# Score products of two heads against zero-padded low keys, and one buffer for the turned attention output

## The chip, the cores and the metric

One core of one Trainium2 chip. The metric is the device time of one execution of the kernel in microseconds (us). In the profile, PE is TensorE (PEld its weight loads), DVE is VectorE, ACT is ScalarE, POOL is GpSimd and SP (SPq its queue of DMA issues) is SyncE.

## What is computed

Two transformer layers over x of 4 sequences, 256 tokens, 256 channels, in fp32. Each layer adds an attention and an FFN, both of the layer norm of the same x:

```python
x = L0_attn_seq
xn = _layernorm(x, axis=-1)
x = x + _L0_attn_ref(xn, ...) + _L0_ffn_ref(xn, ...)
xn = _layernorm(x, axis=-1)
x = x + _L1_attn_ref(xn, L1_attn_w_qkv, L1_attn_w_o) + _L1_ffn_ref(xn, L1_ffn_w_fc, L1_ffn_w_proj)
```

The layer-1 attention is where the change is. It has 32 query heads and 4 key heads of 64 channels:

```python
qkv = jnp.einsum('bsh,oh->bso', hidden_states, w_qkv).reshape(b, s, HQ + 2 * HKV, D)
q, k = _rope(q, pos), _rope(k, pos)                 # x1*cos - x2*sin, x2*cos + x1*sin
k, v = jnp.repeat(k, rep, axis=2), jnp.repeat(v, rep, axis=2)
scores = jnp.einsum('bqhd,bkhd->bhqk', q, k) * D ** (-0.5)
scores = jnp.where(causal[None, None], scores, jnp.finfo(scores.dtype).min)
attn = jax.nn.softmax(scores, axis=-1)
out = jnp.einsum('bhqk,bkhd->bqhd', attn, v).reshape(b, s, HQ * D)
return jnp.einsum('bso,ho->bsh', out, w_o)
```

## The kernel before, in words

**Split numbers.** TensorE multiplies in fp32r, which keeps fewer bits than fp32. So each operand is held as a high part (rounded to fp32r) and a low part (the rest), and products are made of hi·hi, lo·hi and hi·lo. For the scores the two parts of a query lie above each other in 128 partitions: `qT[i]` holds, for each of the 8 heads of a key group, 64 rows of high and 64 rows of low queries. `kT[b % 2]` holds each key head twice above each other, once as high (s = 0) and once as low keys (s = 1). One product with s = 0 gives (q_hi + q_lo)·k_hi, one with s = 1 gives (q_hi + q_lo)·k_lo.

**Units.** The layer-1 attention runs over 16 iterations (batch i // 4, key group i % 4), each with 8 heads and two halves of 128 query tokens. An iteration has 6 units of one score bank (512 columns): u = 0, 1, 4, 5 have two heads of the second half of the queries and 256 keys; u = 2, 3 have four heads of the first half, which by causality need only the first 128 keys. `scores(n)` (line 1232) makes 4 products of 256 columns for a second-half unit and 8 products of 128 columns for a first-half unit (line 1250), and then one mask product (line 1253). The mask is added by a bf16 product with the identity.

**What follows a unit.** DVE takes the negated maxima (line 911), ACT the exponentials in place with their sums (line 515), DVE divides (lines 921 and 927), PE turns the probabilities (line 1004), ACT and DVE split them (lines 524 and 933), PE multiplies them with the values (line 1287) into one bank, ACT and DVE split that (lines 529 and 939) into `oT`, and `project_out` (line 1291) multiplies it with the output weights (line 1307). Every engine has its order written out by `slot(n)`: PE's slot has the scores of unit n, the turning of unit n-2, a group of value products, at u = 0, 3 (and 4 for keys and values) the projection of a coming block ("fill"), and at u = 1 and 5 the output projection of the iteration before. The two halves of `oT` are written from group products in slots u = 4, 5 of the same iteration and u = 0, 2 of the next. Before the change `oT` has a buffer for even and one for odd iterations.

**How queries and keys get ready.** A block is half an iteration's queries (4 heads, two heads above each other in 128 partitions, 2 x 256 columns) or a batch's keys. PE projects it (line 1200), ACT copies it to `raw` (line 490), SP turns the halves of each head with 4 transfers into `turned` (lines 357 and 358), POOL multiplies with cos and sin (`rope_products`, lines 658 and 660) and makes high sum, full sum and low part (`rope_sums`, lines 668 to 670), SP places them by transfers: 4 for a query block (line 378), 8 for a key block (line 381, since keys stand twice). SP's loop is: turn block n+1, then place block n. POOL's list (lines 676 to 702) has between the blocks the low parts of the layer-1 weights (line 606), two a block until block 7, and in the FFN the inverse roots (line 592). The blocks in order are k(0), q(0,0), q(0,1), q(1,0), q(1,1), q(2,0), q(2,1), q(3,0), k(1), q(3,1), q(4,0) and so on; q(i,0) is needed by unit (i,0), q(i,1) by unit (i,3), k(b) by the first unit of batch b. k(b+1) is filled in unit 4 of a batch's second iteration, the values in unit 4 of its third.

**Memory.** Buffers are placed by hand in SBUF; many share their place with others that are dead by then. `probT_hi` lies at 104K, `rope_a` and `rope_b` have two halves of 2 KB each, `split_hi` and `split_lo` too.

**The stages in time.** Layer 0 and the layer-1 norms to about 40 us, the layer-1 FFN to about 90 us (ten steps; blocks are filled in steps 0, 1, 3, 4, 6), attention from there, with units (0,0) and (0,1) inside the FFN's last steps.

Of the kernel before, what the change touches and what calls it, by code (L numbers as in the profile page):

```python
# [7 lines left out]
F32 = mybir.dt.float32  # L8
F32R = mybir.dt.float32r
# [5 lines left out]
P = 128  # L15
# [50 lines left out]
def build(nc, seq, w_qkv0, w_out0, pm, w_ffn0, bias0, w_qkv1, w_o1, w_fc, w_proj, vec, const, out):  # L66
    with ExitStack() as ctx:
# [36 lines left out]
        def at(name, offset, shape, dt=F32):  # L104
# [23 lines left out]
        oT = [[at(f"oT{i}_{w}", k * K + 4 * K * j, [P, 4, SEQ], F32R) for j, w in enumerate(("hi", "lo"))]  # L128
              for i, k in enumerate((148, 64))]
# [7 lines left out]
        probT = [at(f"probT_{w}", k * K, [P, 4, 512], F32R) for w, k in (("hi", 104), ("lo", 112))]  # L137

        yT_full = at("yT_full", 156 * K, [P, B, 512])
        split = [at(f"split_{w}", 156 * K + 4 * K * i, [P, 2, 2, SEQ], F32R) for i, w in enumerate(("hi", "lo"))]  # L140

        rope_a = at("rope_a", 164 * K, [P, 2, 512])
        rope_b = at("rope_b", 168 * K, [P, 2, 512])
# [17 lines left out]
        ones_r = at("ones_r", 185 * K, [P, P], F32R)  # L161
        wcol = at("wcol", 186 * K, [P, DIM])
        idle_in = at("idle_in", 187 * K, [P, 512], BF16)
# [30 lines left out]
        v_zero = sem("v_zero")  # L194
# [48 lines left out]
        def moves(n):  # L243
            return 8 if BLOCKS[n][0] == "k" else 4
# [49 lines left out]
        def group_place(it, i):  # L294

            c, j = unit_heads(GROUPS[i][0])[0], 2 * (i // 2)
            return [w[:, j:j + 2, P * c:P * c + P] for w in oT[it % 2]]
# [29 lines left out]
        def _(sp):  # L327
# [32 lines left out]
            def place_heads(n):  # L360
# [37 lines left out]
        def _(act):  # L398
# [45 lines left out]
            act.wait_ge(ld["cst"], 16)  # L444
            nc.scalar.activation(ones_r[:, :], cst[:, C_ONE:C_ONE + P], ACT.Copy).then_inc(ones_done, 1)
# [106 lines left out]
            for step in range(STEPS):  # L552
# [25 lines left out]
        def _(pool):  # L578
# [8 lines left out]
            pool.wait_ge(zeroed, 3)  # L587

# [62 lines left out]
            def rope_products(n):  # L651
# [4 lines left out]
                whole, half, a, z = (t[:, n % 2, :].rearrange("p (j t) -> p j t", j=2) for t in (raw, turned, rope_a, rope_b))  # L656
                pool.wait_ge(raw_done, n + 1)
                pool.tensor_tensor(a, whole, cos, ALU.mult)  # L658
# [727 lines left out]
```

## Time and profile before

| | us |
|---|---|
| three timed runs: median, lowest, highest | 386.6, 385.39, 388.68 |
| the profiled execution itself | 387.23 |
| its span, first to last instruction | 385.4 |
| PE, DVE, POOL, ACT busy | 369.0, 307.1, 279.4, 250.0 |
| mean granted clock of TensorE | 0.996 |

Durations below are of the profiled execution. Matmuls overlap in the records, so the mean duration of one (some 280 ns) is not its pace; the pace is read from the start of one group to the start of the next. An "idle before" names what ended the wait. SPq rows are DMA issues, not the transfers.

### The profile page before, as it was taken

How to read it: one execution, taken by the hardware profiler on the slowest of the kernel's cores; microseconds unless marked ns; L12 is line 12 of the kernel's file. 1: busy time of each engine (PE TensorE's matmuls, PEld its weight loads, DVE VectorE, ACT ScalarE, POOL GpSimd, SP SyncE). 2: the span in 40 equal slices, each digit the busy share in tenths (PEclk: the TensorE clock that was granted, in tenths of full speed). 3: DMA queues.
4: the chain of work that ended last, by engine and by line, in shares of the span. 5: the costliest groups of instructions: out<-in, count | busy, mean ns of one | idle time of the engine just before them, and what ended most of it. 6: DMA issues, size and time to landing. Idle time of an engine off the chain costs nothing.

```text
span 385.4 us, 8456 instructions
## 1 busy us (share of the span) xinstructions
PE 369.0 (96%) x2888; PEld 343.6 (89%) x2888; DVE 307.1 (80%) x684; ACT 250.0 (65%) x804; POOL 279.4 (72%) x238
## 2 busy tenths in 40 slices
PE   8998889989999998999999999999999999999995
PEld 3667779979899997999999999999999999998985
DVE  6878999876999885779777888787788879788882
ACT  1368855573987764667667676757666667767671
POOL 3437759789999996977779897667997777776000
PEclk9999999999999999899999999999999999999999
DMA  7996112513444345443345643334565343333300
GB/s 261 414 408 284 27 30 55 138 43 81 110 99 96 79 108 130 112 109 80 87 110 120 157 110 92 93 92 98 131 149 142 93 104 83 84 83 86 79 2 27
DMA packets 34219, 45.15 MB, mean 117 GB/s; under 512 B 5505, under 2 KB 25986, under 8 KB 33794
## 3 DMA queue, kind: packets, MB, share of 16 engines
q1 hardware_dynamic: 34032, 44.62, 43.1%
q8 instruction: 23, 0.38, 0.4%
q14 instruction: 18, 0.15, 0.1%
q10 hardware_dynamic: 146, 0.00, 0.0%
HBM read 13.14 MB, written 1.05 MB: 37 GB/s over the span
## 4 chain that ended last, share of the span: by engine, by line
PE 67%; POOL 15%; DVE 9%; SPq 3%; DMA 2%; ACT 2%; issue 2%; POOLq 0%
PE bank L1287 14%; PE bank L1250 11%; PE bank L1307 10%; PE bank L1004 10%; PE bank L1200 10%; PE bank L1253 3%; POOL woT_lo L606 3%; POOL rope_a L669 2%; POOL split_lo L670 2%; POOL split_hi L668 2%; POOL rope_b L660 2%; PE bank L1013 2%; DMA wq0T<-in_L_attn_w_qkv_dram 2%; PE bank L1159 2%; POOL rope_a L658 2%
## 5 line engine op out<-in xcount | busy, mean ns | idle before, releaser
L515 ACT ACTIVATE bank<-bank,neg_max 128x256 f32<-128x256 f32 (+1 forms) x256 | 101.3, 397 | 10.0 <-DVE neg_max L911 9.9
L524 ACT ACTIVATE probT_hi<-bank 128x512 fp32r<-128x512 f32 x96 | 57.6, 600 | 73.6 <-PE bank L1004 73.4
L911 DVE TENSOR_REDUCE neg_max<-bank 128x2 f32<-128x512 f32 (+1 forms) x96 | 65.9, 687 | 31.2 <-PE bank L1253 30.9
L1287 PE MATMUL bank<-probT_hi,v 128*128 128x256 f32 x384 | 76.4, 295 | 0.6 <-DVE oT_lo L939 0.6
L660 POOL TENSOR_TENSOR rope_b<-turned,cst 128x512 f32<-128x512 f32 x36 | 47.1, 1308 | 40.6 <-DMA turned<-raw 40.6
L1250 PE MATMUL bank<-kT,qT 128*128 128x256 f32 (+1 forms) x512 | 73.4, 276 | 1.7 <-DMA qT<-split_lo 1.7
L927 DVE TENSOR_TENSOR prob<-bank,rsum 128x512 f32<-128x512 f32 x96 | 66.4, 691 | 3.3
L1250 PEld LDWEIGHTS bank<-kT,qT 128*128 128x128 f32 x512 | 66.5, 191 | 1.9 <-DMA qT<-split_lo 1.9
L933 DVE TENSOR_TENSOR probT_lo<-bank,probT_hi 128x512 fp32r<-128x512 f32 x96 | 65.4, 681 | 0.5 <-ACT probT_hi L524 0.4
L1287 PEld LDWEIGHTS bank<-probT_hi,v 128*128 128x128 f32 x384 | 58.6, 189 | 3.5 <-issue 2.2
L1004 PE MATMUL bank<-cst,prob 128*128 128x128 f32 x384 | 58.4, 275 | 2.2 <-DVE prob L927 2.2
L1287 PE MATMUL bank<-probT_lo,v 128*128 128x256 f32 x192 | 54.1, 282 | 0.0
L515 ACT ACTIVATION_READ_ACCUMULATOR bank<-bank,neg_max 128x1 f32 x256 | 53.6, 210 | 0.0
L1004 PEld LDWEIGHTS bank<-cst,prob 128*128 128x128 f32 x384 | 46.1, 142 | 5.5 <-DVE prob L927 3.1
L670 POOL TENSOR_TENSOR split_lo<-rope_a,split_hi 128x512 fp32r<-128x512 f32 x36 | 46.3, 1286 | 2.8
L668 POOL TENSOR_TENSOR split_hi<-rope_a,rope_b 128x512 fp32r<-128x512 f32 x36 | 46.2, 1284 | 2.6
L669 POOL TENSOR_TENSOR rope_a<-rope_a,rope_b 128x512 f32<-128x512 f32 x36 | 47.0, 1306 | 0.0
L658 POOL TENSOR_TENSOR rope_a<-raw,cst 128x512 f32<-128x512 f32 x36 | 46.4, 1290 | 0.0
L939 DVE TENSOR_TENSOR oT_lo<-bank,oT_hi 128x256 fp32r<-128x256 f32 x64 | 27.2, 425 | 17.6 <-ACT oT_hi L529 17.3
L1287 PEld LDWEIGHTS bank<-probT_lo,v 128*128 128x128 f32 x192 | 36.3, 189 | 0.0
L1253 PE MATMUL bank<-mask_b,ident_b 128*128 128x256 bf16 (+1 forms) x96 | 30.8, 321 | 0.0
L1200 PE MATMUL bank<-xT_hi,qkvT_hi 128*128 128x256 f32 x144 | 30.7, 295 | 0.0
(158 smaller groups left out, 735.2 us busy)
## 6 DMA issues: line engine op xcount, KB each, us to landing
turned<-raw SPq DMA_DIRECT2D x144, 64.0 KB, 2.0
qT<-split_hi SPq DMA_DIRECT2D x64, 128.0 KB, 2.4
qT<-split_lo SPq DMA_DIRECT2D x64, 128.0 KB, 2.4
wq0T<-in_L_attn_w_qkv_dram SPq DMA_DIRECT2D x4, 512.0 KB, 7.9
wout<-in_L_attn_w_out_dram SPq DMA_DIRECT2D x4, 512.0 KB, 12.4
nat_qkv<-in_L_attn_w_qkv_dram SPq DMA_DIRECT2D x2, 1024.0 KB, 20.5
nat_o<-in_L_attn_w_o_dram SPq DMA_DIRECT2D x1, 2048.0 KB, 21.4
kT<-split_hi SPq DMA_DIRECT2D x16, 128.0 KB, 2.4
```

Of the source, the lines that this page charges most:

```text
L515: ins = nc.scalar.activation(own, own, ACT.Exp, bias=neg_max[it % 2][:, first + j:first + j + 1], accum_out=sums[it % 2][:, first + j:firs ...
L524: nc.scalar.activation(probT[0][:, n % 4, :], bank[2 + n % 2][:, :], ACT.Copy).then_inc(t_hi, 1)
L658: pool.tensor_tensor(a, whole, cos, ALU.mult)
L660: own_done(pool.tensor_tensor(z, half, sin, ALU.mult))
L669: own_done(pool.tensor_tensor(a, a, z, ALU.add))
L911: dve.tensor_reduce(neg_max[n // UNITS % 2][:, unit_columns(n % UNITS)], score_bank(n)[:, :].rearrange("p (h k) -> p h k", h=heads), AX.X, ...
L927: dve.tensor_tensor(a, e, share, ALU.mult).then_inc(s_norm, 1)
L933: dve.tensor_tensor(lo, bank[2 + n % 2][:, :], hi.bitcast(F32), ALU.subtract).then_inc(t_lo, 1)
L1004: ins = pe.transpose(ps[:, P * j:P * j + P], a, ident)
L1200: ins = pe.matmul(bank[place][:, SEQ * j:SEQ * j + SEQ], qkvT[w][:, k, at:at + P], xT[s][:, k, SEQ * b:SEQ * b + SEQ], start=i == 0, stop= ...
L1250: pe.matmul(ps[:, keys * j:keys * j + keys], qT[it % 2][:, h + j, P * c:P * c + P], kT[b % 2][:, g, s, 0:keys], start=j == 0 and s == 0, s ...
L1287: ins = pe.matmul(group_bank(), v[b % 2][:, DH * z:DH * z + P], p, start=m == 0, stop=m == last)
```

## The change

Four of the eight products of a first-half unit (those with the low keys, s = 1) go. In their place stand two products of 256 columns: the stationary operand is `q_hi`, the high queries of two heads above each other as the rope leaves them, the moving one `k_pad`, which for z = 0 has the low keys in rows 0 to 63 and zeros below, and for z = 1 zeros above and the low keys in rows 64 to 127. So 128 columns come out for each of the two heads. The product of low queries with low keys is left out in first-half units.

For that `rope_sums` writes the high queries into `q_hi[it % 2]` instead of `split_hi`; POOL waits before it until the scores that read the old ones are done. The key blocks get 4 more transfers (12 in all), which place the low keys of the first 128 tokens in `k_pad`. POOL zeroes each `k_pad` once with two fills (`pad(0)` at the start, `pad(1)` behind the FFN's last root). PE waits for the zeroing in first-half units of the first two batches. `rope_a`, `rope_b` and `split_hi` have one buffer, and `rope_products` waits for the low part of the block before. `oT` has one buffer, `probT_hi` moves to 64K, and `ones_r` (moved from ScalarE's early work to FFN step 3), `wcol` and `idle_in` get other places.

```diff
-        oT = [[at(f"oT{i}_{w}", k * K + 4 * K * j, [P, 4, SEQ], F32R) for j, w in enumerate(("hi", "lo"))]
-              for i, k in enumerate((148, 64))]
+        oT = [at(f"oT_{w}", (148 + 4 * j) * K, [P, 4, SEQ], F32R) for j, w in enumerate(("hi", "lo"))]
+        q_hi = [at(f"q_hi{i}", k * K, [P, HG // 2, SEQ], F32R) for i, k in enumerate((168, 104))]
+        k_pad = [at(f"k_pad{i}", k * K, [P, HKV, 2, P], F32R) for i, k in enumerate((184, 108))]
...
-        probT = [at(f"probT_{w}", k * K, [P, 4, 512], F32R) for w, k in (("hi", 104), ("lo", 112))]
+        probT = [at(f"probT_{w}", k * K, [P, 4, 512], F32R) for w, k in (("hi", 64), ("lo", 112))]
...
-        split = [at(f"split_{w}", 156 * K + 4 * K * i, [P, 2, 2, SEQ], F32R) for i, w in enumerate(("hi", "lo"))]
-
-        rope_a = at("rope_a", 164 * K, [P, 2, 512])
-        rope_b = at("rope_b", 168 * K, [P, 2, 512])
+        split_hi = at("split_hi", 156 * K, [P, 2, SEQ], F32R)
+        split_lo = at("split_lo", 158 * K, [P, 2, 2, SEQ], F32R)
+        rope_a = at("rope_a", 164 * K, [P, 2, SEQ])
+        rope_b = at("rope_b", 166 * K, [P, 2, SEQ])
...
         def moves(n):
-            return 8 if BLOCKS[n][0] == "k" else 4
+            return 12 if BLOCKS[n][0] == "k" else 4
...
                 for w in range(2):
-                    for s in range(2):
-                        src = split[s][DH * w:DH * w + DH, n % 2, :, :].bitcast(F32)
+                    own = slice(DH * w, DH * w + DH)
+                    low = split_lo[own, n % 2, :, :].bitcast(F32)
+                    if what == "q":
+                        high = q_hi[it % 2][own, 2 * half:2 * half + 2, :].bitcast(F32)
+                    else:
+                        high = split_hi[own, :, :].bitcast(F32)
+                    for s, src in enumerate((high, low)):
                         if what == "q":
                             sp.dma_start(qT[it % 2][DH * s:DH * s + DH, 4 * half + w:4 * half + 4:2, :].bitcast(F32), src).then_inc(placed[n % 2], 16)
                         else:
                             for z in range(2):
                                 sp.dma_start(kT[b % 2][DH * z:DH * z + DH, w:HKV:2, s, :].bitcast(F32), src).then_inc(placed[n % 2], 16)
+                    if what == "k":
+                        for z in range(2):
+                            sp.dma_start(k_pad[b % 2][DH * z:DH * z + DH, w:HKV:2, z, :].bitcast(F32), low[:, :, 0:P]).then_inc(placed[n % 2], 16)
...
-            act.wait_ge(ld["cst"], 16)
-            nc.scalar.activation(ones_r[:, :], cst[:, C_ONE:C_ONE + P], ACT.Copy).then_inc(ones_done, 1)
...
+                if step == WCOL_STEP - 2:
+                    act.wait_ge(ld["cst"], 16)
+                    act.wait_ge(lo0_done, B)
+                    nc.scalar.activation(ones_r[:, :], cst[:, C_ONE:C_ONE + P], ACT.Copy).then_inc(ones_done, 1)
...
+            def pad(i):
+
+                for z in range(2):
+                    own = k_pad[i][DH * (1 - z):DH * (1 - z) + DH, :, z, :]
+                    pool.memset(own.bitcast(F32), 0.0).then_inc(pad_zero, 1)
+                    pool.wait_ge(pad_zero, 2 * i + z + 1)
+
+            pool.wait_ge(v_zero, 2)
+            pool.wait_ge(blk_done, 1)
+            pad(0)
...
                 pool.wait_ge(raw_done, n + 1)
-                pool.tensor_tensor(a, whole, cos, ALU.mult)
+                if n:
+                    pool.wait_ge(split_done, n)
+                pool.tensor_tensor(rope_a[:, :, :], whole, cos, ALU.mult)
...
-                hi, lo = (t[:, n % 2, :, :] for t in split)
+                a, z, lo = rope_a[:, :, :], rope_b[:, :, :], split_lo[:, n % 2, :, :]
+                if BLOCKS[n][0] == "k":
+                    hi = split_hi[:, :, :]
+                else:
+                    _, it, part = BLOCKS[n]
+                    hi = q_hi[it % 2][:, 2 * part:2 * part + 2, :]
+                    if it >= 2:
+                        pool.wait_ge(s_full, (it - 2) * UNITS + 3 + part)
...
             tile_root(7)
+            pool.wait_ge(root_out, TILES + B + 2)
+            pad(1)
             rope_products(3)
...
                 c, heads, h, keys = unit_heads(u)
+                if c == 0 and n < HKV * UNITS * 2:
+                    pe.wait_ge(pad_zero, 2 * (b + 1))
                 for j in range(heads):
-                    for s in range(2):
+                    for s in range(c + 1):
                         pe.matmul(ps[:, keys * j:keys * j + keys], qT[it % 2][:, h + j, P * c:P * c + P], kT[b % 2][:, g, s, 0:keys],
                                   start=j == 0 and s == 0, stop=False, skip_group_check=True)
+                    if c == 0 and j % 2:
+                        pe.matmul(ps[:, keys * (j - 1):keys * (j + 1)], q_hi[it % 2][:, (h + j) // 2, 0:P], k_pad[b % 2][:, g, :, :],
+                                  start=False, stop=False, skip_group_check=True)
```

## Rows read from the trace of the kernel before

**Rows 1.** The page: busy shares, and two of its costliest groups.

```profile
PE 369.0 (96%) x2888; PEld 343.6 (89%) x2888; DVE 307.1 (80%) x684; ACT 250.0 (65%) x804; POOL 279.4 (72%) x238
...
L1250 PE MATMUL bank<-kT,qT 128*128 128x256 f32 (+1 forms) x512 | 73.4, 276 | 1.7 <-DMA qT<-split_lo 1.7
...
L670 POOL TENSOR_TENSOR split_lo<-rope_a,split_hi 128x512 fp32r<-128x512 f32 x36 | 46.3, 1286 | 2.8
```

**Rows 2.** Busy time of each engine in two stretches.

```profile
134.00:144.00 10.00, 10.00 (x86) 9.83 (x86) 8.74 (x18) 6.62 (x25) 9.76 (x8) 1.00 0.46 107
...
200.00:220.00 20.00, 20.00 (x172) 19.68 (x171) 16.51 (x34) 13.49 (x48) 17.61 (x15) 1.00 0.57 133
```

**Rows 3.** Chain of waits in order of time: start, duration, what.

```profile
137.61 1.31 POOL split_lo L670
...
138.94 0.65 SPq L381
...
144.29 0.57 SPq L357
...
145.54 1.72 SPq L357
...
150.02 2.36 DMA qT<-split_lo
...
152.42 1.14 PE bank L1250 x8
...
168.74 0.84 PE bank L1250 x8
...
186.16 0.84 PE bank L1250 x8
```

**Rows 4.** Timeline of TensorE around the gap.

```profile
150.44 0.28 PE L1287 MATMUL bank<-probT_lo,v 128*128 128x256 f32 x1
152.42 1.14 PE L1250 MATMUL bank<-kT,qT 128*128 128x128 f32 x8 [1.71 <-DMA qT<-split_lo]
...
157.03 0.64 PE L1250 MATMUL bank<-kT,qT 128*128 128x256 f32 x4
```

**Rows 5.** Stretch behind the gap; granted clock behind POOL's busy time.

```profile
153.30:156.80 3.50, 3.50 (x19) 3.30 (x18) 2.14 (x4) 1.89 (x9) 3.49 (x3) 0.51 0.35 82
```

**Rows 6.** Timeline of all engines, iteration 7.

```profile
217.59 0.64 PE L1250 MATMUL bank<-kT,qT 128*128 128x256 f32 x4
...
218.07 0.28 PE L1253 MATMUL bank<-mask_b,ident_b 128*128 128x256 bf16 x1
...
223.26 1.01 PE L1250 MATMUL bank<-kT,qT 128*128 128x128 f32 x8
...
224.10 0.39 PE L1253 MATMUL bank<-mask_b,ident_b 128*128 128x512 bf16 x1
...
227.61 0.68 DVE L911 TENSOR_REDUCE neg_max<-bank 128x4 f32<-128x512 f32 x1
```

**Rows 7.** Timeline of TensorE, iteration 14, behind its first-half units.

```profile
353.50 0.66 PE L1004 MATMUL bank<-cst,prob 128*128 128x128 f32 x4 [0.69 <-DVE prob L927]
```

**Rows 8.** Timeline of GpSimd, start and end of the FFN.

```profile
1.78 0.52 POOL L581 MEMSET probT<- 1x512 f32 x1
...
10.86 3.45 POOL L592 TENSOR_TENSOR tok<-tok,neg_half 128x8 f32<-128x8 f32 x2 [6.48 <-DVE tok L750]
...
79.84 0.54 POOL L592 TENSOR_TENSOR ffac<-ffac,neg_half 128x1 f32<-128x1 f32 x1 [1.70 <-DVE ffac L717]
```

**Rows 9.** Timeline of SyncE's queue: last issues of q(4,0) and q(7,1).

```profile
156.63 0.62 SPq L378 DMA_DIRECT2D qT<-split_lo  x1
...
219.17 0.61 SPq L378 DMA_DIRECT2D qT<-split_lo  x1
```

**Rows 10.** Timeline of TensorE: scores of units (4,0) and (7,3).

```profile
162.91 0.64 PE L1250 MATMUL bank<-kT,qT 128*128 128x256 f32 x4
...
226.20 1.01 PE L1250 MATMUL bank<-kT,qT 128*128 128x128 f32 x8
```

More of the change, by code:

```diff
@@ L160, in build @@
         pmT = at("pmT", 184 * K, [P, 2, 2, HC])
-        ones_r = at("ones_r", 185 * K, [P, P], F32R)
-        wcol = at("wcol", 186 * K, [P, DIM])
-        idle_in = at("idle_in", 187 * K, [P, 512], BF16)
+        ones_r = at("ones_r", 162 * K, [P, P], F32R)
+        wcol = at("wcol", 163 * K, [P, DIM])
+        idle_in = at("idle_in", 136 * K, [P, 512], BF16)
         abs_out = at("abs_out", 164 * K, [P, FF // P * DIM])
@@ L193, in build @@
         out_full, out_added = sem("out_full"), sem("out_added")
-        v_zero = sem("v_zero")
+        v_zero, pad_zero = sem("v_zero"), sem("pad_zero")
         raw_done, rope_done, split_done = sem("raw_done"), sem("rope_done"), sem("split_done")
@@ L296, in group_place @@
             c, j = unit_heads(GROUPS[i][0])[0], 2 * (i // 2)
-            return [w[:, j:j + 2, P * c:P * c + P] for w in oT[it % 2]]
+            return [w[:, j:j + 2, P * c:P * c + P] for w in oT]
         def group_bank():
@@ L655, in rope_products @@
                 cos, sin = (cst[:, a:a + SEQ].rearrange("p (j t) -> p j t", j=1).to_broadcast([P, 2, SEQ]) for a in (at, at + SEQ))
-                whole, half, a, z = (t[:, n % 2, :].rearrange("p (j t) -> p j t", j=2) for t in (raw, turned, rope_a, rope_b))
+                whole, half = (t[:, n % 2, :].rearrange("p (j t) -> p j t", j=2) for t in (raw, turned))
                 pool.wait_ge(raw_done, n + 1)
-                pool.tensor_tensor(a, whole, cos, ALU.mult)
+                if n:
+                    pool.wait_ge(split_done, n)
+                pool.tensor_tensor(rope_a[:, :, :], whole, cos, ALU.mult)
                 pool.wait_ge(turn_landed[n % 2], 64 * (n // 2 + 1))
-                own_done(pool.tensor_tensor(z, half, sin, ALU.mult))
+                own_done(pool.tensor_tensor(rope_b[:, :, :], half, sin, ALU.mult))
             def rope_sums(n):
@@ L665, in rope_sums @@
                     has_landed(pool, n - 2)
-                a, z = (t[:, n % 2, :].rearrange("p (j t) -> p j t", j=2) for t in (rope_a, rope_b))
-                hi, lo = (t[:, n % 2, :, :] for t in split)
+                a, z, lo = rope_a[:, :, :], rope_b[:, :, :], split_lo[:, n % 2, :, :]
[6 more added lines that the diff above has]
+                        pool.wait_ge(s_full, (it - 2) * UNITS + 3 + part)
                 pool.tensor_tensor(hi, a, z, ALU.add)
@@ L1306, in project_out @@
                             final = g == HKV - 1 and half == 1 and e == 1 and (s, w) == (0, 1) and j == 3
-                            ins = pe.matmul(bank[BANK_OUT][:, DIM * e:DIM * e + DIM], oT[it % 2][s][:, j, e:e + 2 * P - 1:2],
+                            ins = pe.matmul(bank[BANK_OUT][:, DIM * e:DIM * e + DIM], oT[s][:, j, e:e + 2 * P - 1:2],
                                             woT[w][:, 4 * g + j, :], start=first, stop=final, skip_group_check=True)
```

## The prediction

> **What bounds the kernel now.** I read the page's busy shares first, then the chain that ended last, then the stretches, then the timelines of the one place where the chain changes engine. A unit is written (i,u): iteration i of 16 (batch i//4, key group i%4), u from 0 to 5; k(b) and q(i,half) are the blocks that the rope prepares.
>
> TensorE (PE) is busy 96% of the span [rows 1], and in the steady stretch all of it: 20.00 of 20 us from 200 to 220 [rows 2]. But the chain has three parts. Up to 80 us it is the FFN. From 80 us to 139 us it is GpSimd (POOL): 9.76 of 10 us busy in 134 to 144 [rows 2], no pause longer than the 0.07 us between a result and its reader, because the rope of each block (five operations of 1.29 us [rows 1]) and two weight splits of the same size take some 9.2 us, while PE makes a block each 8.7 us (half of 186.16 - 168.74, one iteration [rows 3]). Its last link is k(1)'s split, which ends at 138.92. Then the SyncE queue (SP) issues eight transfers of k(1), four turns, and the four of q(3,1), and only when the last of these lands does PE go on: 150.02 + 2.36 = 152.4 [rows 3]. PE's preceding product started at 150.44 and the scores of (3,3) at 152.42, after 1.71 us of idling [rows 4]; that is the only time in 512 score products that PE waited for queries [rows 1]. From 152.4 on the chain is PE itself.
>
> Behind that gap the granted clock was 0.51 from 153.3 to 156.8, about the lower level of 1.2 GHz [rows 5], and PE's pace is the full one again from 157.03 [rows 4]: 3.4 us at half speed, which lost about 1.7 us. So a microsecond saved on PE ahead of 150 is eaten by the gap, one saved behind it counts, and one added to POOL from 86 us on or to SP in 139 to 150 is paid in full.
>
> **The change, part by part.**
>
> *Products.* A first-half unit (u = 2, 3; two per iteration, 32 in all) has eight score products of 128 columns. They run from 223.26 to 224.10, when the mask product starts: 0.84 us, 105 ns each [rows 6]. A product of 256 columns takes 120 ns: four from 217.59 to 218.07 [rows 6]. After the change a unit has four of 128 and two of 256: 4 x 105 + 2 x 120 = 660 ns, 0.18 us less. Bounds: if all six run at 120 ns it is 0.12, if all at 105 it is 0.21. No row shows 128- and 256-column products mixed; I take 0.18, since the weight load of the next product can lie beside a longer stream.
> The Trainium skill, TensorE: Matmul & The Clock Gate, section LDWEIGHTS, gives a weight load as columns/1.2 ns, an estimate of 107 ns for 128 columns, and under Back-to-back issue gap 109 ns for a warm 256-column product alone. By that the unit would save 0.21 us, the upper bound; the 120 ns of the row speak for less.
>
> Of the 32 units, 7 stand ahead of the gap: (0,2) to (3,2). They save 1.3 us, and PE then waits that much longer. 25 stand behind it: 25 x 0.18 = 4.5 us. Two of these, (14,3) and (15,3), have no projection beside them, and PE waits there for VectorE's normalising anyway (0.69 us at 353.50 [rows 7]); I drop them: -0.4. VectorE is close in first-half slots too: its maxima at 227.61 start without a pause behind the oT work [rows 6]. I give 0.3 us of the gain back for that. Left: 3.8 us (bounds 2.3 and 5.2).
>
> *k_pad zeroing.* Two fills of 64 partitions x 512 numbers per buffer. A fill of 512 numbers per partition took 0.52 us [rows 8]; with 0.07 behind each and 0.07 for the wait on the root: 1.2 us per pad (bounds 0.7, if a fill takes half of that row, and 2.2, if it takes double; spans on POOL are rough). pad(0) lies in POOL's idle 6.48 us before 10.86 [rows 8]: nothing. pad(1) stands behind the last root, at 86 us, in the stretch where POOL is the chain: +1.2 in full. Behind it on POOL are all ropes and weight splits to k(1), and for these SP and PE wait.
>
> *Four more transfers per k block.* Eight issues take SP from 138.94 to 144.29, 0.67 us each [rows 3]: +2.7 us per k block. For k(0) this shifts the turn of q(0,1), before a stretch where POOL idles 1.70 us until 79.84 [rows 8]: nothing. For k(1) the four stand ahead of the turn of q(4,0) and of q(3,1)'s placing, on the chain: +2.7 in full (bounds 2.5 and 3.8, the latter with a further slow issue). One of the four turn issues took 1.72 us [rows 3], 1.1 more than the others, a hitch that few issues have; it has even odds to fall elsewhere: -0.5.
>
> *Clock.* PE's idle time before (3,3) grows from 1.7 to 1.7 + 1.2 + 2.7 + 1.3 - 0.5 = 6.4 us. A half-clock stretch behind it is there already; how it falls can change its price from 1.7 to between 0.8 and 3.4. I take no change, and keep -0.9 and +1.7.
> The same page of the skill, section Terms, prices it as throttled time x (1 - K/N): 3.4 x 0.5 = 1.7 us, as the row shows; its rule that idle PE loses the clock speaks against this change, since by it a longer gap never costs less than a gap too short to lose it.
>
> *Without a price.* One oT buffer: the heads of iteration i are written behind PE's own products of its slot, and the reader of the old ones (the output projection of i-1) is issued on PE before them in (i,1) and (i,5); no wait is new. rope_a and rope_b single: POOL runs in order, the added wait is for its own last operation, 0.07 us, and between 86 and 139 us a weight split lies between. q_hi as the source and its wait on scores: those units were issued before the fill whose block is roped. ones_r on ScalarE moves from beside PE's work to step 3 of the FFN, behind a wait of ScalarE's for PE. probT_hi over the spent projT: its first write follows the last projection on PE. Waits on pad_zero: set long before.
>
> *Later blocks.* q(4,0)'s last issue is at 156.63, its landing some 2.4 later at 159.0, its scores at 162.91 [rows 9, 10]: 3.9 us to spare, and SP and PE shift together. q(7,1), behind k(2), is issued last at 219.17, lands at 221.6, and is needed at 226.20 [rows 9, 10]: 4.6 us to spare, of which the four issues take 2.7 and PE's three faster units on the way 0.5. 1.4 us stay; the like holds behind k(3).
>
> **Sum** against the profiled execution's own 387.23 us (span 385.4, 1.8 around it): + 1.2 + 2.7 - 0.5 - 3.8 = -0.4, so 386.8. That execution is 0.6 above the median of the three timed runs (386.6), so 386.2.
>
> **Rivals.**
> 1. *The preparation hides* (the gap does not grow): 25 units of 0.18 count and neither fills nor issues do: 386.6 - 4.5 = 382.1. For it: q blocks other than q(3,1) landed in time. Against: POOL has no pause from 86 to 139, and SP issues back to back from there to 150.
> 2. *The queue starves PE at each new batch* (the other side): behind k(2) and k(3) the spare 1.4 us are used up as well. It decides from 1.4 us on, for instance by one slow issue and a later k split. Each gap then costs some 1 us and up to 1.7 of clock: 386.2 + 2 x 2.7 = 391.6. For it: the slack of 4.6 is measured and 3.2 of it go. Against: 1.4 us is more than one hitch of 1.1.
> 3. *The products don't pay*: a 256-column product among 128s costs as much as two of them, and the unit saves nothing. Then 386.6 + 1.2 + 2.7 - 0.5 = 390.0. Against: 120 against 2 x 105 ns in the rows.
>
> **How the numbers follow.** Forecast 0.65, its own range 383.0 to 388.8 (gain 2.3 to 5.2, pad 0.7 to 2.2, clock -0.9 to +1.7, not all at once). Rival 1: 0.18; rival 2: 0.08; rival 3: 0.09. 1% is 3.9 us, about what a measurement of this kernel tells from no change: faster is below 382.7, slower above 390.5. Rival 1 gives nearly all of faster, with a little of the forecast: 0.18. Rival 2 and nearly half of rival 3 give slower: 0.12. Same: 0.70. The range reaches down to rival 1 and up towards rival 3: 382.0 to 390.0.
>
> **What would show it.** Right: eight-product score groups of first-half units become six in 0.66 us; twelve kT and k_pad issues behind k(1)'s split, which ends near 140.1; (3,3) starting at 155 to 156.5 behind 5 to 7 us of idle PE, then half clock; a period of 17.0 instead of 17.4 us afterwards; no gap at (7,3) and (11,3). Wrong: (3,3) near 152, or a PE gap in front of another unit, or no shorter period.

## The result: 0.9% slower, and where the time went

The changed kernel takes 390.17 us (median of 20 runs, 387.27 to 393.82); the kernel before took 386.56 us beside it (20 runs, 385.05 to 388.68). The ratio is 1.0092, with a 95% interval of 1.0073 to 1.0111; one execution of the changed kernel, more than 1.5% above its fastest (393.82), is left out of the ratio. The forecast was 386.2 us with a range from 382.0 to 390.0. The profiled execution took 391.75 us, its span is 389.9 us, 4.5 more than before; it is 1.6 us above the median of the twenty, so what is read from it below explains the longer ones among them.

The page of the changed kernel: busy time of the engines, the granted clock over the span, the chain by engine, and the group of the score products.

```profile
span 389.9 us, 8377 instructions
...
PE 365.6 (94%) x2808; PEld 339.6 (87%) x2824; DVE 307.5 (79%) x684; ACT 250.6 (64%) x804; POOL 282.1 (72%) x242
...
PEclk9999999999999998799999999999999899999999
...
POOL 40%; PE 32%; issue 12%; DVE 8%; SPq 3%; ACT 2%; DMA 1%; POOLq 0%
...
L1284 PE MATMUL bank<-kT,qT 128*128 128x256 f32 (+1 forms) x384 | 63.7, 275 | 7.4 <-DMA qT<-split_lo 7.4
```

PE is busy 3.4 us less than before [rows 1] and the span is longer. The last line says why: PE idled 7.4 us for placed queries where it idled 1.7 before [rows 1]. The clock row has two dents. PE's waits for queries in the changed kernel, from the view of waits (us in total, times, longest):

```profile
PE bank L1284 <- DMA qT<-split_lo: 7.4, 3, 5.1
```

Three waits instead of one, and the timeline of PE in the changed kernel shows them at (3,3), (7,3) and (11,3), each the first unit that reads the query block placed behind a k block:

```profile
149.84 0.28 PE L1324 MATMUL bank<-probT_lo,v 128*128 128x256 f32 x1
155.25 0.69 PE L1284 MATMUL bank<-kT,qT 128*128 128x128 f32 x2 [5.13 <-DMA qT<-split_lo]
...
228.82 0.44 PE L1284 MATMUL bank<-kT,qT 128*128 128x128 f32 x2 [0.20 <-DMA qT<-split_lo]
...
301.96 0.44 PE L1284 MATMUL bank<-kT,qT 128*128 128x128 f32 x2 [2.04 <-DMA qT<-split_lo]
```

Setting each unit's first score product against the same unit of the kernel before gives a ledger (both from the timeline of PE; shift = after - before, us):

```
unit          before   after    shift   what happened since the row above
(3,2)         147.62   147.18   -0.44   cheaper products ahead of the gap
(3,3)         152.42   155.25   +2.83   idle 5.13 instead of 1.71
(3,4)         157.03   160.41   +3.38   more of it at half clock
(7,2)         223.26   225.69   +2.43   six first-half units cheaper
(7,3)         226.20   228.82   +2.62   idle 0.20, (7,2) cheaper
(11,2)        295.36   296.98   +1.62   cheaper products
(11,3)        298.30   301.96   +3.66   idle 2.04
(12,0)        307.11   312.24   +5.13   half clock behind (11,3)
(15,5)        371.36   375.52   +4.16   cheaper products
```

So up to (11,2) the change goes nearly as forecast: each first-half unit earns 0.16 us behind the gap, and (7,3) loses 0.35. A gap costs 0.15 us more than the idle time says (at (3,3) before, (7,3) and (11,3)), since the records of products overlap. At (11,3) all that was earned behind (3,4) is lost again and more. The clock behind the first gap, in windows of the changed kernel (length, then busy time and count of PE, PEld, DVE, ACT and POOL, the granted clock, DMA share and GB/s):

```profile
153.00:155.20 2.20, 0.00 (x0) 0.00 (x0) 0.00 (x0) 0.00 (x0) 2.12 (x3) 0.59 0.84 194
155.20:160.00 4.80, 4.75 (x21) 4.46 (x22) 2.14 (x4) 1.76 (x8) 4.58 (x4) 0.50 0.40 93
```

The clock fell while PE was still idle, and stayed at its lower level (1.2 GHz) for about 6.8 us in all, until 160.0. From (3,3) to (3,4) the kernel before took 4.61 us and this one 5.16. Behind (11,3) it is about 3.4 us of half clock, and the shift grows by 1.5 from there to (12,0).

How often the clock falls differs between executions. A stretch of 3.4 us at half clock takes 0.004 off the mean granted clock of a span of 385 us. Of 75 executions of the kernel before that ran beside the experiments, 41 have 0.998 or more, so no such stretch, and a median of 385.3 us; 22 have 0.995 or 0.996 like the profiled one (387.1), and 12 have 0.991 (388.4). Of the changed kernel's twenty none is above 0.991: ten lie at 0.989 to 0.991 (mean 388.6 us), which leaves room for little more than the 6.8 us at (3,3), and ten at 0.983 to 0.987 (391.5 us, the profiled one among them), which have a further stretch.

**The chain at (3,3).** POOL first, in the changed kernel: the two fills, then the first rope behind them, and k(1)'s last split.

```profile
86.05 1.09 POOL L604 MEMSET k_pad<- 64x512 f32 x2
87.22 1.30 POOL L682 TENSOR_TENSOR rope_a<-raw,cst 128x512 f32<-128x512 f32 x1
...
138.51 1.29 POOL L700 TENSOR_TENSOR split_lo<-rope_a,split_hi 128x512 fp32r<-128x512 f32 x1
```

The rope starts 1.19 later than before (86.03); the split ends at 139.80 instead of 138.91, +0.89. Then the queue of SP:

```profile
139.83 1.33 SPq L387 DMA_DIRECT2D kT<-split_hi  x2
...
145.13 1.73 SPq L387 DMA_DIRECT2D kT<-split_lo  x2
146.90 1.27 SPq L390 DMA_DIRECT2D k_pad<-split_lo  x2
148.27 0.57 SPq L358 DMA_DIRECT2D turned<-raw  x1
...
152.87 0.62 SPq L384 DMA_DIRECT2D qT<-split_lo  x1
```

Twelve issues take 8.44 us where eight took 5.35 [rows 3]: four more at 0.65, and one slow one (the pair at 145.13 takes 1.73). The slow turn of [rows 3] is gone (-1.1). The last issue is 2.85 later than the 150.02 of [rows 3], and the scores follow it.

**The chain at (7,3).** The last placing of q(7,1) is issued at 225.09, 5.92 us later than before [rows 9], while PE stands 2.43 later. Its time from issue to landing, in the changed kernel and in the one before:

```profile
DMA to landing us min/median/max: 3.7/3.7/3.7
```

```profile
DMA to landing us min/median/max: 3.4/3.4/3.4
```

Before the change it landed at 222.6 and was needed at 226.20: 3.6 us to spare. The queue takes 5.92 - 2.43 = 3.5 of that and the landing 0.3 more, so PE waits 0.2.

**The chain at (11,3).** The same queue, first in the changed kernel:

```profile
284.76 2.11 SPq L387 DMA_DIRECT2D kT<-split_hi  x2
...
298.11 0.61 SPq L384 DMA_DIRECT2D qT<-split_lo  x1
298.77 1.90 SPq L400 DMA_DIRECT2D out_dram<-x  x1
```

and in the kernel before:

```profile
290.96 0.61 SPq L378 DMA_DIRECT2D qT<-split_lo  x1
291.62 0.60 SPq L391 DMA_DIRECT2D out_dram<-x  x1
```

The last placing is issued 7.15 us later while PE stands only 1.62 later. Three parts can be read: the four issues (2.6), a slow issue in the first pair (2.11 against 1.33, 0.8), and k(3)'s split, whose end moved from 280.96 to 284.73. The split is late because the turned half of q(11,0) landed late. The timeline of POOL in the changed kernel:

```profile
272.81 1.28 POOL L684 TENSOR_TENSOR rope_b<-turned,cst 128x512 f32<-128x512 f32 x1 [3.44 <-DMA turned<-raw]
```

In the kernel before it started at 269.22, behind 2.30 us of idling. The last turn of q(11,0) was issued at 267.13 before and at 269.25 after; those 2.1 us are nearly PE's own shift there (1.9), and the other 1.5 passed between this issue and its landing. From there the lateness runs on through two blocks: the split +3.77, the four issues and the slow one +3.4, together the 7.15.

And the placed queries land later: the times from issue to landing of q(11,1)'s last placings, in the changed kernel and in the one before, are

```profile
DMA to landing us min/median/max: 2.7/3.3/3.8
```

```profile
DMA to landing us min/median/max: 2.3/2.5/2.6
```

The store of batch 1's output (line 400) is issued 0.66 us behind the last placing in both kernels; the last placing issued at 298.11 lands at 301.9, 3.8 later. Before, it was issued at 290.96, landed 2.6 later at 293.6 and was needed at 298.30: 4.7 us to spare. The queue takes 7.15 - 1.62 = 5.5 of that and the landing 1.2, in all 6.7: 2.0 us short, which is the gap.

### The profile page after: what moved, and what is told of

Same layout as the page of the kernel before. It is cut to its first block, busy times and chain, and to the rows that moved or that the text cites. A ratio compares the mean times of both kernels' runs of the same rounds, so it can differ in the third digit from the quotient of the medians.

```text
span 389.9 us, 8377 instructions
## 1 busy us (share of the span) xinstructions
PE 365.6 (94%) x2808; PEld 339.6 (87%) x2824; DVE 307.5 (79%) x684; ACT 250.6 (64%) x804; POOL 282.1 (72%) x242
## 3 DMA queue, kind: packets, MB, share of 16 engines
HBM read 13.14 MB, written 1.05 MB: 36 GB/s over the span
## 4 chain that ended last, share of the span: by engine, by line
POOL 40%; PE 32%; issue 12%; DVE 8%; SPq 3%; ACT 2%; DMA 1%; POOLq 0%
POOL split_lo L700 8%; POOL rope_b L684 8%; POOL rope_a L699 8%; POOL q_hi L698 7%; POOL rope_a L682 6%; PE bank L1324 5%; PE bank L1036 5%; PE bank L1344 4%; PE bank L1232 3%; PE bank L1284 3%; PE bank L1191 2%; PE bank L1167 2%; PE bank L1068 2%; PE bank L1045 2%; SPq L387 1%
## 5 line engine op out<-in xcount | busy, mean ns | idle before, releaser
L1284 PE MATMUL bank<-kT,qT 128*128 128x256 f32 (+1 forms) x384 | 63.7, 275 | 7.4 <-DMA qT<-split_lo 7.4
L1284 PEld LDWEIGHTS bank<-kT,qT 128*128 128x128 f32 x384 | 55.8, 194 | 8.0 <-DMA qT<-split_lo 8.0
L698 POOL TENSOR_TENSOR q_hi<-rope_a,rope_b 128x512 fp32r<-128x512 f32 x32 | 41.6, 1299 | 2.3
L700 POOL TENSOR_TENSOR split_lo<-rope_a,q_hi 128x512 fp32r<-128x512 f32 x32 | 41.2, 1287 | 2.5
L497 ACT ACTIVATE raw<-bank 128x512 f32<-128x512 f32 x36 | 21.7, 604 | 14.7 <-PE bank L1232 13.3
```

Of the source, the lines that this page charges most:

```text
L698: pool.tensor_tensor(hi, a, z, ALU.add)
L700: pool.tensor_tensor(lo, a, hi.bitcast(F32), ALU.subtract).then_inc(split_done, 1)
L1284: pe.matmul(ps[:, keys * j:keys * j + keys], qT[it % 2][:, h + j, P * c:P * c + P], kT[b % 2][:, g, s, 0:keys], start=j == 0 and s == 0, s ...
```

## The experiments

Every ratio below is against the kernel before, run on the same chip beside the experiment. Its medians there were 386.78 (e1 to e4), 385.38 (e5 to e8) and 387.07 us (e9 to e12). The gaps are those of the one profiled execution of each kernel.

**Is it the queue alone?** e1 takes the kernel before, with its eight products, its buffers and no fill, and puts four transfers of 32 KB that nobody reads behind k(1), k(2) and k(3) on SP.

```diff
-            return 8 if BLOCKS[n][0] == "k" else 4
+            return 12 if BLOCKS[n][0] == "k" and BLOCKS[n][1] else 8 if BLOCKS[n][0] == "k" else 4
...
+                    if what == "k" and b:
+                        for z in range(2):
+                            sp.dma_start(spare[DH * z:DH * z + DH, w, :, :], split[1][DH * w:DH * w + DH, n % 2, :, 0:P // 2].bitcast(F32)).then_inc(placed[n % 2], 16)
```

> The kernel before with four more transfers behind k(1), k(2) and k(3) on SyncE's queue (copies of low keys to a spare place; each 32 KB instead of 64), nothing else changed. Theory Q (the queue is on the chain at the first new batch): unit (3,3) starts 2.7 us later, its idle time grows from 1.7 to 4.4 us, and no other unit waits, since (7,3) and (11,3) had 3 us to spare: 386.6 + 2.7 = 389.3 us, or up to 1 more by the clock. Rival H (the transfers hide): 386.6, (3,3) near 152.4.

It took 390.08 us, ratio 1.0097 (1.0059 to 1.0135). The timeline of PE in e1:

```profile
154.84 1.55 PE L1254 MATMUL bank<-kT,qT 128*128 128x128 f32 x8 [4.23 <-DMA qT<-split_lo]
```

(3,3) starts 2.42 us later than before, its span is 2.5 longer, and PE waits nowhere else for queries. The four issues are on the chain at (3,3) at about their own length, though these carry half as much. That (7,3) and (11,3) have no gap in this execution shows that the issues alone needn't use up the slack there: the last placing of q(7,1) is issued at 224.85 here, nearly as late as in the changed kernel (225.09), and lands in 2.4 us instead of 3.7.

**e2: the same keys, later.** Two transfers out of `kT`, behind the next query block, replace the four.

```diff
-                    if what == "k":
-                        for z in range(2):
-                            sp.dma_start(k_pad[b % 2][DH * z:DH * z + DH, w:HKV:2, z, :].bitcast(F32), low[:, :, 0:P]).then_inc(placed[n % 2], 16)
+            def pad_keys(n):
+                b = BLOCKS[n][1]
+                has_landed(sp, n)
+                for z in range(2):
+                    own = slice(DH * z, DH * z + DH)
+                    sp.dma_start(k_pad[b % 2][own, :, z, :].bitcast(F32), kT[b % 2][own, :, 1, 0:P].bitcast(F32)).then_inc(pad_placed, 16)
...
                 place_heads(n)
+                if n and BLOCKS[n - 1][0] == "k":
+                    pad_keys(n - 1)
```

> The changed kernel, but k_pad is filled by two transfers out of kT, issued behind the placing of the next query block, instead of four in the key block's own placing. Theory Q: (3,3) starts 2.7 us earlier, near 152.6; q(11,1) is placed 2.7 us earlier, so the gap of 2.0 us in front of (11,3) and the half-clock stretch behind it (1.7 us) go: 390.2 - 2.7 - 3.6 = 383.9 us. Rival H: no change, 390.2. Rival P (the gaps come from the padding's fills on GpSimd and the added wait for the low part): (3,3) stays later than 154 and the time above 388.

385.55 us, ratio 0.9958 (0.9931 to 0.9984). PE in e2:

```profile
153.31 0.69 PE L1293 MATMUL bank<-kT,qT 128*128 128x128 f32 x2 [3.15 <-DMA qT<-split_lo]
```

The gap at (3,3) falls from 5.13 to 3.15 us, those at (7,3) and (11,3) are gone. The change with two late issues in place of its four early ones is faster than before. It is 1.7 us short of the expectation (383.9): one turn was issued slowly again (1.69 us), (3,3) starts at 153.31 and not near 152.6, and the half clock at the gap stayed at 6.8 us. In three of its twelve executions (382.8 to 383.4 us) the granted clock was 0.999, so no half clock followed there.

**e3: the fills, later.** `pad(1)` goes from behind the last root to behind q(3,1)'s rope.

```diff
-            pool.wait_ge(root_out, TILES + B + 2)
-            pad(1)
             rope_products(3)
...
                 weights_lo(2 * n + 2, min(2 * n + 4, len(W_UNITS)))
+                if BLOCKS[n] == ("q", 3, 1):
+                    pool.wait_ge(split_done, n + 1)
+                    pad(1)
```

> The changed kernel, but the two fills of the second k_pad stand behind the rope of q(3,1), where GpSimd waits 4.3 us for a turned block, instead of behind the last root of the FFN. Theory: GpSimd is the chain from 86 to 140 us, so k(1)'s split ends 1.1 us earlier and (3,3) starts 1.1 us earlier: 389.1 us. Rival (the fills were hidden, the queue alone sets (3,3)): 390.2, (3,3) at 155.2.

388.42 us, ratio 1.0059 (1.0026 to 1.0092): less than the change's 1.0092, though the intervals overlap. The idle time at (3,3) is 4.30 instead of 5.13, nearly the 0.89 that the fills had put on k(1)'s split. Even so (3,3) starts at 155.88 and not 1.1 us earlier than in the changed kernel, because this execution has a half-clock stretch in the FFN; e12 below has the same one, and against it k(1)'s first issue is 1.04 earlier (140.28 and 141.32) and (3,3) 0.91.

**e4: the store, later.** The output store goes one query block back, so that it isn't issued right behind the placing that PE waits for.

```diff
-                if BLOCKS[n][0] == "q" and BLOCKS[n][2] == 1 and BLOCKS[n][1] in (7, 11, 15):
-                    b = BLOCKS[n][1] // HKV - 1
+                if BLOCKS[n] in (("q", 8, 0), ("q", 12, 0), ("q", 15, 1)):
+                    b = {8: 0, 12: 1, 15: 2}[BLOCKS[n][1]]
```

> The changed kernel, but the store of a finished batch is issued one query block later, not right behind the placing of q(7,1) and q(11,1). Theory L (the store beside it slows the landing of the last placed queries from 2.4 to 3.8 us): they land in 2.4 us, the gap in front of (7,3) goes, that in front of (11,3) shrinks from 2.0 to 0.6 us and with luck keeps the clock: between 387.2 and 388.8 us. Rival: landing stays 3.8 us, 390.2.

389.31 us, ratio 1.0068 (1.004 to 1.0096), above the 387.2 to 388.8 of theory L and not told apart from the change. In the profile (7,3) has no gap and (11,3) one of 0.71 us with no fall of the clock, but (3,3) idled 5.83. The landings speak against the theory. With no store behind it, q(7,1)'s last placing still took 3.3 us to land, here with the turn that now follows it on SP:

```profile
225.24 0.62 SPq L384 DMA_DIRECT2D qT<-split_lo  x1
225.95 1.40 SPq L358 DMA_DIRECT2D turned<-raw  x1
```

q(11,1)'s landed in 2.4. In e12 below, an execution of the changed kernel itself, it landed in 2.4 with the store right behind it. So a late landing needs no store, and the store doesn't always bring one.

**e5: the three together** (e2, e3 and e4 in one kernel, no other edit).

> The changed kernel with the three shifts at once: k_pad by two late transfers out of kT, the second k_pad's fills behind q(3,1)'s rope, the store one block later. Theory: against the kernel with late k_pad transfers alone (385.55) the fills take 1.1 us off the gap of 3.15 us in front of (3,3), the store nothing, since (11,3) had no gap there: 384.4 us, half-clock stretch unchanged. Rival (the gap in front of (3,3) is SyncE's alone): 385.5.

383.75 us, ratio 0.9945 (0.9924 to 0.9966), near the 384.4 expected. The idle time at (3,3) is 2.04, as reckoned (3.15 - 1.1); the half-clock stretch, expected unchanged, is 3.4 us and not 6.8 in the profiled execution.

**e6: and fewer issues for the keys themselves.** On top of e5, high and low parts of a key block lie in one tensor, and `kT` has the head last but one, so that one transfer per z and w carries both parts: four issues per k block.

```diff
-        split_hi = at("split_hi", 156 * K, [P, 2, SEQ], F32R)
-        split_lo = at("split_lo", 158 * K, [P, 2, 2, SEQ], F32R)
+        split_all = at("split_all", 156 * K, [P, 3, 2, SEQ], F32R)
+        split_hi, split_lo = split_all[:, 0, :, :], split_all[:, 1:3, :, :]
...
-        kT = [at(f"kT{i}", k * K, [P, HKV, 2, SEQ], F32R) for i, k in enumerate((172, 140))]
+        kT = [at(f"kT{i}", k * K, [P, 2, HKV, SEQ], F32R) for i, k in enumerate((172, 140))]
...
+                        both = split_all[own, 0:2 + n % 2:1 + n % 2, :, :].rearrange("p s j t -> p s (j t)").bitcast(F32)
+                        for z in range(2):
+                            sp.dma_start(kT[b % 2][DH * z:DH * z + DH, :, 2 * w:2 * w + 2, :].rearrange("p s j t -> p s (j t)").bitcast(F32), both).then_inc(placed[n % 2], 16)
```

> As the kernel with the three shifts, and the keys placed by four transfers that carry high and low part together instead of eight, with kT laid out for it. Theory Q: SyncE's queue is 2.7 us shorter at k(1) again, (3,3) is ready when TensorE comes to it, its gap (some 2 us) and the half-clock stretch behind it go, and TensorE runs at its own pace throughout: (3,4) starts near 152.2, and the time is 379.1 us, at most 381 if (4,0) now waits a little for q(4,0). Rival C (TensorE loses its clock there anyway, or GpSimd takes the queue's place): 382 or more.

380.74 us, ratio 0.9884 (0.9856 to 0.9913): 1.6 us above the 379.1 expected, below the rival's 382. PE in e6, at (3,3) and (3,4):

```profile
150.79 0.44 PE L1297 MATMUL bank<-kT,qT 128*128 128x128 f32 x2 [0.59 <-DMA qT<-split_all]
...
153.68 0.64 PE L1297 MATMUL bank<-kT,qT 128*128 128x256 f32 x4
```

The wait is 0.59 us, and the next unit follows 2.89 us later, at full clock, so this gap cost no more than itself. (3,4) was expected near 152.2 and starts at 153.68. Some issues were slow here too (three of 1.05 to 1.13 us behind the keys).

**e7: the fused keys without the change.** The kernel before, with its two split tensors made one in the same way and four issues per k block; all products are the old ones.

> The kernel before, with keys placed by four transfers instead of eight and nothing else changed. Theory Q: the queue is 2.7 us shorter at k(1), the gap of 1.7 us and the half-clock stretch behind it (1.7 us) go: 386.7 - 3.4 = 383.3 us. Rival (the gap is GpSimd's lateness, not the queue's length): 386.7.

384.57 us, ratio 0.9969 (0.9951 to 0.9987); the profiled execution took 383.88, 3.35 less than that of the kernel before. PE in e7:

```profile
150.62 1.11 PE L1252 MATMUL bank<-kT,qT 128*128 128x128 f32 x8
```

No wait stands at (3,3), so profile against profile the gap of [rows 4] and its half clock were worth 1.7 + 1.7, as the prediction had them. The times say less: the ratio is a gain of 1.2 us, against the 3.4 expected, in part because many executions of the kernel before have no half clock to lose. Among those at 0.998 or more the medians are 385.3 and 384.1.

**e8: the products undone in e6.** The order, buffers, fills and transfers of e6, with eight products per first-half unit; `k_pad` is filled and not read.

```diff
-                    for s in range(c + 1):
+                    for s in range(2):
...
-                    if c == 0 and j % 2:
-                        pe.matmul(ps[:, keys * (j - 1):keys * (j + 1)], q_hi[it % 2][:, (h + j) // 2, 0:P], k_pad[b % 2][:, 2 * (g % 2) + g // 2, :, :],
-                                  start=False, stop=False, skip_group_check=True)
```

> As the kernel with late and fused transfers, but first-half units make the old eight products of 128 columns; k_pad is filled and not read. The new products are worth 0.16 us per unit by the starts of the units. Theory: with no gap left every one of them counts, 31 x 0.16 = 4.9 us more than the same kernel with the new products: 384.0 us if that one takes 379.1. Rival (only part counts, because VectorE or the queues hide it): less than 3 us between the two.

384.51 us, ratio 0.9974 (0.9958 to 0.999), so the products are worth 3.8 us in e6 (384.51 - 380.74). The expectation of 4.9 counted 31 units; those ahead of (3,3) count little while PE still waits there in e6, and (14,3) and (15,3), where PE waits for VectorE, count less too. How the missing 1.1 us divides wasn't measured. e8 also prices the rest of the change: it has the single buffers, `q_hi`, the moved `ones_r` and `probT_hi`, the fills and the late padding, and with the old products it takes as long as the kernel before with fused keys (e7: 384.57 us), which has none of them. So none of these costs anything that the times show.

**e9: weight splits, later.** In the changed kernel the last two of the weight splits, which stand in POOL's stretch without a pause, go behind the ropes of q(3,1) and q(4,0).

```diff
-                weights_lo(2 * n + 2, min(2 * n + 4, len(W_UNITS)))
+                weights_lo(2 * n + 2, min(2 * n + 4, len(W_UNITS) - 2))
+                if n in (9, 10):
+                    weights_lo(n + 7, n + 8)
```

> The changed kernel, but the last two weight splits (2.6 us of GpSimd) stand behind the ropes of q(3,1) and q(4,0) instead of ahead of k(1)'s. Theory: GpSimd is the chain up to k(1)'s split whatever it does there, so the split ends 2.6 us earlier, (3,3) starts near 152.7, and the time is 390.2 - 2.6 = 387.6 us; the gap in front of (11,3) stays, since that one hangs on TensorE's own pace and the queue. Rival (only SyncE's queue counts): 390.2.

387.44 us, ratio 1.0019 (0.9991 to 1.0046), an interval below the change's. k(1)'s first issue is 2.44 us earlier than in the changed kernel and (3,3) 1.98 (a turn took 1.44), behind 3.31 us of idling instead of 5.13: POOL is the first link of the chain, as [rows 2] had it. The time is the expected 387.6, but in part for another reason: the gap at (11,3), which was expected to stay, is absent in this execution.

**e10: all of it** (e6 with e9's edit; `pad(1)` ahead of the late weight splits).

> The kernel with late and fused transfers (380.7), and the last two weight splits behind the ropes of q(3,1) and q(4,0). Theory: the last 0.6 us of waiting in front of (3,3) go and nothing else waits: 380.1 us. Rival (q(4,0), later by the moved work, is now late for (4,0)): 381 or more.

379.65 us, ratio 0.9831 (0.9804 to 0.9859): 1.7% faster than before and, by the two ratios, 2.6% than the change (0.9831/1.0092). The page of e10, then PE at (3,3):

```profile
span 377.7 us, 8356 instructions
...
PE 360.1 (95%) x2808; PEld 335.6 (89%) x2824; DVE 307.1 (81%) x684; ACT 250.5 (66%) x804; POOL 282.9 (75%) x242
...
PE 81%; DVE 11%; ACT 4%; DMA 2%; issue 1%; POOL 0%; SPq 0%
```

```profile
150.02 0.34 PE L1299 MATMUL bank<-kT,qT 128*128 128x128 f32 x2
```

PE doesn't wait for queries here or anywhere, and the mean granted clock of this execution is 0.999. POOL is out of the chain (0%, against 40% in the change), and PE carries 81% of it.

**e11 and e12: how firm is the gap at (11,3)?** The changed kernel again, one execution each.

> The changed kernel itself once more, for its gaps. If the gap of 2.0 us in front of (11,3) belongs to the kernel's order, it is there again within 0.5 us, with half clock behind it. If it is made by slow issues and landings that differ from execution to execution, it is 0 to 1 us here or the time differs by 3 us.

> The same again: gap in front of (11,3) within 0.5 us of 2.0 if it belongs to the order, otherwise different from the other look.

They took 391.37 and 390.49 us. PE's waits for queries in e11, then in e12:

```profile
PE bank L1284 <- DMA qT<-split_lo: 7.3, 3, 5.2
```

```profile
PE bank L1284 <- DMA qT<-split_lo: 6.3, 3, 5.2
```

All three gaps are there each time. (3,3) is steady (5.13, 5.18, 5.15), (7,3) small (0.20, 0.39, 0.30), and (11,3) varies: 2.04, 1.76, 0.80. The clock fell behind it in the first two and not in the third. By the measure set beforehand (within 0.5 us of 2.0) e11 speaks for the order of the work and e12 for the execution. What varies is the landing of the last placing: 3.8, 3.4 and 2.4 us. Here are (11,3) in e12, the store behind that placing, and its landing:

```profile
302.20 0.44 PE L1284 MATMUL bank<-kT,qT 128*128 128x128 f32 x2 [0.80 <-DMA qT<-split_lo]
```

```profile
300.42 0.59 SPq L400 DMA_DIRECT2D out_dram<-x  x1
```

```profile
DMA to landing us min/median/max: 2.4/2.4/2.4
```

With a landing of 2.4 us the gap is 0.80 (0.71 in e4): at least that much was there in all three executions. The rest, up to 1.2 us, and the half clock with it, come with the landing and differ between executions. A single profile with that gap at 0 (e3, e9) shows less than it seems to.

## Why the prediction was wrong

Its own terms, in its order:

- **Products.** Confirmed. Iteration 10 of the changed kernel shows the six of a first-half unit, and the mask product that follows:

```profile
281.44 0.34 PE L1284 MATMUL bank<-kT,qT 128*128 128x128 f32 x2
281.61 0.33 PE L1287 MATMUL bank<-k_pad,q_hi 128*128 128x256 f32 x1
281.78 0.33 PE L1284 MATMUL bank<-kT,qT 128*128 128x128 f32 x2
281.95 0.33 PE L1287 MATMUL bank<-k_pad,q_hi 128*128 128x256 f32 x1
282.13 0.39 PE L1290 MATMUL bank<-mask_b,ident_b 128*128 128x512 bf16 x1
```

  Six take 0.69 us (281.44 to 282.13) instead of 0.84 [rows 6], and the shifts of the ledger fall by 0.16 per unit (behind (12,0) by 0.12 on average, where (14,3) and (15,3) are among the eight); the prediction took 0.18. All told they gave 3.6 us behind (3,3), forecast 3.8; in e6 against e8 3.8. Rival 3 (products don't pay) is out.
- **Fills and four issues at (3,3).** The fills measured 1.09 us and their delay 1.19 (forecast 1.2), of which 0.89 reached k(1)'s split. The issues measured 2.6 plus a slow one (0.45), the slow turn didn't come back. Together the last issue moved by 2.85 and the scores of (3,3) by 2.83, against a forecast of 1.2 + 2.7 - 0.5 = 3.4. e1's issues alone gave 2.42. Rival 1 (the preparation hides) is out.
- **Single buffers, `q_hi`, `ones_r`, `probT_hi`: no price.** Borne out: e8 has all of them with the old products and takes what e7 takes without them (384.51 and 384.57 us).
- **"I take no change" for the clock**: wrong by 0.7 us at (3,3), within the bound of +1.7. Before, 4.61 us from (3,3) to (3,4) with a gap of 1.71; after, 5.16 with two cheaper products and a gap of 5.13. At full clock the unit takes 2.94 before and 2.78 after, so the half clock cost 1.67 and now 2.38. This is profile against profile. In the medians the term is larger, since over half of the executions of the kernel before lose no clock there and none of the changed ones is free of it.
- **"4.6 us to spare [...] 1.4 us stay; the like holds behind k(3)"**: this step failed. Three things were wrong in it. First, the landing. The prediction took q(7,1) to land some 2.4 us after its last issue, the median of all placings; in the trace of the kernel before that one took 3.4, so 3.6 us were to spare and not 4.6. Second, at (7,3) the draw on the slack was about right (3.5 us of queue against PE, forecast 2.7 + 0.5), so with the right landing the step would have left 0.4 us, and the landing's further 0.3 and the rest of the queue made it a miss of 0.20. Third, "the like" doesn't hold behind k(3): there the queue fell back by 5.5 us against PE (the four issues 2.6, a slow pair 0.8, the late turned half of q(11,0) 1.5, small pieces 0.6), and the landing took 1.2 longer, against 4.7 to spare. PE had by (11,2) gained 1.8 us on its start at (3,4) (3.38 - 1.62), since its products are cheaper: a faster PE comes to the same place with less slack.

Rival 2, given a chance of 0.08, is what happened in kind: the queue starves PE behind k(2) and k(3). In number it was not. It priced each of the two gaps at 2.7 us, 5.4 in all; they cost 0.35 and 3.83 in the profiled execution, of which 1.6 is half clock, and about half of the twenty executions have no more half clock than that at (3,3). That its 391.6 lies near the 390.17 measured, and nearer the profiled 391.75, is partly luck.

The whole ledger, profiled execution against profiled execution: +2.83 at (3,3), +0.71 of clock behind it, -3.56 for the products, +0.35 at (7,3) (0.19 of shift and the 0.16 that unit (7,2) saves), +3.83 at (11,3) (from +1.62 to +5.13, with 0.32 of savings between), and +0.34 behind (15,5) that I can't place: +4.5. The forecast had 3.4 - 3.8 = -0.4. Of the difference of 4.9, (11,3) alone is 3.8: 2.2 for the gap and 1.6 of half clock.

What the page and chain said before was right: e1, e3 and e9 each move (3,3) by nearly the price of the link they touch (2.42 of 2.6, 0.91 of 1.1, 1.98 of 2.6 us). The mistake was to work out only the one place where PE already waited, to check the second with a median landing, and to leave the third to "the like".

Some things stay open. Why single issues take 1.1 to 2.1 us instead of 0.6 was not tried. In part they belong to the order of the work: in all three profiled executions of the changed kernel one pair of k(1)'s issues took 1.7 to 1.8 us and the first of k(3)'s 2.1 to 2.2, where a pair mostly takes 1.3, and one placing near 271 us took 1.4 to 1.5. In part they don't: the store behind q(7,1) took 1.81, 0.59 and 1.74 us, the one behind q(11,1) 1.90, 1.55 and 0.59. Late landings mostly came with a slow issue just behind them (3.4 us with 1.58 before; 3.7 with 1.81, 3.8 with 1.90, 3.6 with 1.74 in the changed kernel; 3.3 with 1.40 in e4), and quick ones with quick issues (2.4 with 0.59 in e12). Not always, though: in e11 a landing of 3.8 has an issue of 0.59 behind it and a slow one (1.29) only as the second, and e7 has a landing of 4.2 with no slow issue near it. What delays both is open, and so is why the turned half of q(11,0) lands late. And some executions (those profiled in e3, e8 and e12) have a further half-clock stretch of 3.4 us in the FFN, worth 1.3 to 1.6 us, that no edit explains.

## What to carry to other kernels

A saving on the busiest engine counts only behind the last wait for whatever feeds it. Price every added transfer by where its issue stands in its queue, at some 0.65 us here for 32 to 256 KB, and work out the slack at every point that repeats the pattern, from the landing that the trace has for that very transfer and not from the median, and with the delays of the steps behind. And where a gap's clock loss comes in some executions only, one profile of each kernel isn't enough to add up a change of 1%. The same products stand in a kernel 0.9% slower than before with twelve issues ahead of the next queries, and in one 1.2% faster (e6) with four fused ones and the padding placed late.

## What was not expected of the hardware

- The cost of an idle gap isn't in proportion to its length. In the profiled executions, gaps of 0.20 to 0.80 us left the granted clock whole. Gaps of 1.7 to 2.04 us were followed by about 3.4 us of half clock (the granted clock of 1.2 GHz), which cost some 1.6. With gaps of 3.15 to 5.83 us (e2, e9, e3 and e4, and the changed kernel's own) there were 6.8 us of half clock; but part of that lay in the gap itself, and behind the gap of 5.13 it cost 2.4. e1's gap of 4.23 was followed by 3.4 only.
- Nor does the same kernel lose its clock each time: 41 of 75 executions of the kernel before, and 3 of e2's 12, had a mean granted clock of 0.998 or more. Whether those had a shorter gap or the same one without the loss isn't known, since no such execution was profiled.
- The size of a transfer didn't show in its issue: e1's 32 KB took a median of 0.61 us, the fused keys of e6 and e7 (64 partitions of 4 KB, 256 KB) 0.66, though their landing took longer (a median of 4.1 us in e7, at most 5.9).
